# Attention in a decoder layer: the weighing of V in two halves, and scores moved ahead of the last third of a slot's transpositions

## The chip, the cores and the metric

The kernel runs on one core of a Trainium2 chip. The metric is device time in microseconds; lower is better. A core has five engines: TensorE (PE; its weight loads are PEld), VectorE (DVE), ScalarE (ACT), GpSimd (POOL) and SyncE (SP), which starts the DMAs.

## The reference

One decoder layer on x of 16 x 224 x 512: a Mamba block, cross-attention to a context of 750 keys, and a feed-forward net with binarised weights. The change is in the attention:

```python
qh = _split_heads(q @ Wq + bq)          # q: layer norm of x, 16 heads of depth 32
kh = _split_heads(k @ Wk + bk)
vh = _split_heads(v @ Wv + bv)
logits = jnp.einsum('bhqd,bhkd->bhqk', qh, kh) / jnp.sqrt(jnp.asarray(DEPTH, dtype=jnp.float32))
logits = logits + mask * NEG_INF_SCALE
attn = jax.nn.softmax(logits, axis=-1)
out = jnp.einsum('bhqk,bhkd->bhqd', attn, vh)
out = out.transpose(0, 2, 1, 3).reshape(B, Sq, D_MODEL)
return out @ Wo + bo
```

## The kernel before

Three phases follow each other: `mamba_phase` (which also makes keys and values and keeps them in DRAM), `attention_phase` and `ffn_phase`. In the attention phase everything is cut into slots, 16 to a batch of 224 queries, 256 in all. Each engine has a program of its own, written as a loop over the slots (L1222 for PE, L1325 for ACT, L1488 for DVE, L1559 for POOL, L1617 for SP), and semaphores tie them together. The order on an engine is the order in that loop; an instruction that waits holds up all behind it.

A slot n is one half (375) of the keys for a block of four heads and 112 queries, so two slots make a block and four slots a group of four heads with all 224 queries. In it:

- PE makes the scores (`scores`, L1136), four matmuls into the PSUM tile `sps`, once the masks of the slot before have read that tile.
- DVE adds the mask, negates, and keeps the minimum (`negate_and_mask`, L1394), four instructions from `sps` into `sc`, one of two buffers that blocks take in turn. Before it writes a block's first half, it waits until PE has transposed all of the block two before (L1401). After the odd slot it makes `nmax`, the maximum over both halves.
- ACT makes the exponentials in place, two a slot (`exponential`, L1282), one for each head of a block. The first of a block needs `nmax`, so it can only start in the odd slot after its masks.
- PE transposes two heads' probabilities two slots later in three parts of four transpositions (`transpose_p(m, pair)`, L1150; here a part is called a third). Two PSUM buffers `tps` take the thirds in turn, so each third waits for the copy of the one before last. ACT copies the first and the last third to `pT`, DVE the middle one (`keep_pT`, L1293 and L1412). The first third needs one of the two heads' exponentials, the others both.

Beside these stand units that share two more PSUM banks `ups` in turn: `project_q` (L1126, one for each group, copied by ACT in `keep_q`), `weigh_v` (L1175, 24 matmuls over all keys of a group; it waits until ACT and DVE have copied all the group's thirds), `spread_sums` (L1167, the reciprocal sums, copied by ACT in `keep_sums`), `out_proj` (L1189, two a batch, added to x by DVE) and `transpose_h` (L1108, the normalised x of the next batch). The layer norm of the next batch runs over four engines: statistics on DVE (`stats_of_x1`), a logarithm and an exponential on ACT (`guess_rsqrt`, L1268), four small instructions on POOL (`rsqrt_of_rows`), and the scaling on DVE (`normalise`, L1375), ahead of which DVE waits.

By slot of a batch, r0 to r15, PE had: Q in r1, r5, r9, r13; a weighing with its sums in r2, r6, r10, r14; an output projection in r4 and r7 (of the batch before); the transpositions of h in r12; nothing beside the scores and the thirds in r0, r3, r8, r11, r15. The order in a slot was scores, first third, Q or weighing, middle third, h, sums or output projection, last third.

## Time and profile before

| | us |
|---|---|
| median of 3 runs | 3591.51 (3588.01 to 3595.86) |
| profiled execution | 3588.75 |
| its span | 3587.4 |
| PE busy in the span | 3224.2 (90%) |
| DVE busy | 2655.8 (74%) |
| ACT busy | 2388.7 (67%) |
| POOL busy | 1806.3 (50%) |

The mean granted clock of TensorE is 0.963 of full speed. In a timeline each line is one instruction, or several alike in a row (x8), with its start and length; the bracket at the end says how long the engine stood still before it and what released it. A matmul in float32 shows as two instructions. The lengths of matmuls overlap, so the price of a unit is read from its start to the start of the next one.

### The profile page before, as it was taken

The numbers are of one execution on the slowest core, as the hardware profiler recorded it, in microseconds if no ns is written. First come the engines' busy times: TensorE is split into PE (matmuls) and PEld (weight loads), VectorE is DVE, ScalarE is ACT, GpSimd is POOL, SyncE is SP. The second block draws the span as 40 slices with busy tenths as digits, with TensorE's granted clock in tenths as the row PEclk, the third lists the DMA queues.
The fourth block names the chain that finished last, engine by engine and source line by source line (L and its number), as shares of the span: only waits on it lengthen the run. The fifth ranks groups of instructions, "written<-read, shape, count | busy, mean of one in ns | idle before, by whom it ended". The sixth has DMA issues, their size and how long they took to land. (4 is left out here: it accounts for less than half of the span.)

```text
span 3587.4 us, 59841 instructions
## 1 busy us (share of the span) xinstructions
PE 3224.2 (90%) x20864; PEld 2259.3 (63%) x20864; DVE 2655.8 (74%) x4671; ACT 2388.7 (67%) x5339; POOL 1806.3 (50%) x1213
## 2 busy tenths in 40 slices
PE   5798989898898988988997998999999999999998
PEld 4566655665566655666554666666666666678787
DVE  2899999999999999999984776767766677622221
ACT  5777788777877788777863667666666667522221
POOL 2778887888878888888873000000000000055554
PEclk8899999999999999999998999999999999999999
DMA  5667666666666666676564041111211121020110
GB/s 166 162 175 196 188 167 157 184 175 188 168 161 182 190 171 160 175 196 180 159 166 155 6 124 59 46 46 65 71 46 46 51 78 66 18 76 24 36 35 24
DMA packets 286234, 425.03 MB, mean 118 GB/s; under 512 B 28689, under 2 KB 226065, under 8 KB 281330
## 3 DMA queue, kind: packets, MB, share of 16 engines
q1 hardware_dynamic: 278573, 411.44, 41.1%
q10 hardware_dynamic: 7365, 9.77, 0.9%
q8 instruction: 170, 2.79, 0.3%
q14 instruction: 126, 1.03, 0.1%
HBM read 320.12 MB, written 101.02 MB: 117 GB/s over the span
## 5 line engine op out<-in xcount | busy, mean ns | idle before, releaser
L810 POOL TENSOR_TENSOR a_hs<-a_rep,a_bmat 128x896 f32<-128x896 f32 x512 | 1061.0, 2094 | 291.0 <-PE a_yps L322 290.7
L442 ACT ACTIVATE a_states<-a_rep,a_a_neg 128x224 f32<-128x224 f32 x2048 | 793.5, 437 | 103.0 <-DVE a_hs L706 101.5
L699 DVE TENSOR_TENSOR_SCAN a_states<-a_states,a_hs 128x900 f32<-128x900 f32 x384 | 779.6, 2030 | 72.7 <-ACT a_states L442 57.9
L1403 DVE CUSTOM_DVE_ANT_0 b_sc<-sps,early_mask 112x375 f32<-112x375 f32 x1024 | 500.0, 545 | 154.1 <-PE sps L1146 153.9
L1162 PEld LDWEIGHTS b_tps<-ident,b_sc 112*125 112x125 f32 x3072 | 402.0, 191 | 286.4 <-issue 168.7
L1162 PE MATMUL b_tps<-ident,b_sc 112*125 112x112 f32 x3072 | 491.4, 289 | 77.3 <-DVE b_pT L1417 36.2
L1289 ACT ACTIVATE b_sc<-b_sc,b_nmax 112x750 f32<-112x750 f32 x512 | 467.4, 914 | 62.5 <-DVE b_nmax L1409 62.3
L1545 POOL TENSOR_SCALAR b_x_var<-mv 112x2 f32<-112x2 f32 x16 | 3.4, 213 | 889.2 <-DVE mv L1454 889.2
L344 PE MATMUL a_work<-early_scan_hT,w_in 128*128 128x224 f32 x2048 | 424.3, 363 | 8.9 <-issue 6.3
L706 DVE TENSOR_TENSOR a_hs<-a_states,a_cmat 128x896 f32<-128x896 f32 x384 | 419.2, 1092 | 13.2
L344 PEld LDWEIGHTS a_work<-early_scan_hT,w_in 128*128 128x128 f32 x2048 | 395.5, 196 | 49.1 <-issue 42.2
L1298 ACT ACTIVATE b_pT<-b_tps 125x448 f32<-125x448 f32 x512 | 272.5, 535 | 135.9 <-PE b_tps L1162 134.7
L399 PE MATMUL a_work<-ctx,a_wk 128*128 128x250 f32 x1536 | 347.8, 379 | 14.3 <-ACT kv_out L489 14.3
L403 PE MATMUL a_work<-wv,ctx 128*125 128x512 f32 x768 | 349.6, 598 | 9.6 <-ACT kv_out L486 8.9
L322 PE MATMUL a_yps<-a_hs,a_fold 128*32 128x224 f32 x4096 | 236.4, 373 | 115.2 <-POOL a_hs L817 46.1
L399 PEld LDWEIGHTS a_work<-ctx,a_wk 128*128 128x128 f32 x1536 | 288.8, 191 | 64.8 <-issue 16.7
L374 PE MATMUL a_work<-a_w_out,a_yT 128*112 128x512 f32 x512 | 255.5, 657 | 33.5 <-DVE early_du L689 33.5
L1779 ACT ACTIVATE c_g<-sps,early_b,early_alpha 128x512 f32<-128x512 f32 x112 | 87.1, 778 | 287.7 <-PE sps L1719 282.5
L699 DVE TENSOR_TENSOR_SCAN a_hs<-a_states,a_hs 128x900 f32<-128x900 f32 x128 | 258.9, 2023 | 24.1 <-ACT a_states L442 24.1
L322 PEld LDWEIGHTS a_yps<-a_hs,a_fold 128*32 128x32 f32 x4096 | 129.9, 113 | 223.9 <-DVE a_hs L706 101.7
L1815 DVE CAST c_gT_hi<-c_g 128x512 fp32r<-128x512 f32 x112 | 61.8, 552 | 278.3 <-ACT c_g L1779 278.3
L1849 POOL TENSOR_TENSOR c_gT_lo<-c_g,c_gT_hi 128x512 fp32r<-128x512 f32 x112 | 146.4, 1309 | 212.9 <-DVE c_gT_hi L1815 212.9
(194 smaller groups left out, 5011.4 us busy)
## 6 DMA issues: line engine op xcount, KB each, us to landing
a_rep<-du_scratch SPq DMA_DIRECT2D x512, 224.0 KB, 5.7
w_in<-W_in_dram SPq DMA_DIRECT2D x128, 512.0 KB, 4.4
du_scratch<-early_du SPq DMA_DIRECT2D x16, 1792.0 KB, 11.5
ctx<-ctxT_dram SPq DMA_DIRECT2D x48, 500.0 KB, 6.0
v_scratch<-kv_out SPq DMA_DIRECT2D x96, 250.0 KB
k_scratch<-kv_out SPq DMA_DIRECT2D x96, 250.0 KB, 4.5
b_keys<-k_scratch SPq DMA_DIRECT2D x8, 1500.0 KB, 8.6
b_v<-v_scratch SPq DMA_DIRECT2D x8, 1500.0 KB
```

The costliest lines, as they stand in the source:

```text
L322: mm = pe.matmul(yps[j * DG:(j + 1) * DG, tile % 2 * L:(tile % 2 + 1) * L], fold[:], hs[(G4 * tile + j) % RING][:, q, 1:ROW], start=(q == ...
L344: mm = pe.matmul(work[:, bank, j * L:(j + 1) * L], w_in[unit % WINS][:, k, j * P:(j + 1) * P], hT[:, k, :], start=(k == 0), stop=(k == KD ...
L399: mm = pe.matmul(work[:, bank, j * WIDE:(j + 1) * WIDE], wk[:, k, (2 * half + j) * P:(2 * half + j + 1) * P], keys[:, k, :], start=(k == 0 ...
L403: mm = pe.matmul(work[0:KC, bank, :], keys[:, k, half * KC:(half + 1) * KC], wv[:, k, :], start=(k == 0), stop=(k == KD - 1))
L442: e = act.activation(rows(states[:, g % DA, :])[:, q, 1:ROW], rep[tile % REPS][:, j, 0, :], ACT.Exp, scale=a_neg[:, g % SLOTS, q:q + 1])
L699: dve.tensor_tensor_scan(state if g % G4 else whole, state, whole, 0.0, ALU.mult, ALU.add).then_inc(S["scan"], 1)
L706: dve.tensor_tensor(hh[:, :, 1:ROW], rows(states[:, g % DA, :])[:, :, 1:ROW], cmat[b % 2][:], ALU.mult).then_inc(S["hc"], 1)
L810: pool.tensor_tensor(hs[g % RING][:, :, 1:ROW], rep[tile % REPS][:, j, 1, :].unsqueeze(1).broadcast_to([P, Q, L]), bmat[b % 2][:], ALU.mul ...
L1162: mm = pe.transpose(tps[0:KC, tile % 2, c * TT:(c + 1) * TT], sc[m // 2 % 2][:, 2 * (m % 2) + head, chunk * KC:(chunk + 1) * KC], ident[0: ...
L1289: act.activation(sc[block % 2][:, j, :], sc[block % 2][:, j, :], ACT.Exp, scale=-1.0, bias=nmax[:, block % 2, j:j + 1], accum_out=esum[:, ...
L1298: act.activation(place(m, pair), transposed(tile), ACT.Copy).then_inc(S["pt_act"], 1)
L1403: dve.tensor_tensor_reduce(out=sc[block % 2][:, j, cols], in0=sps[0:TT, j, 0:HALF], in1=mask[:, block % 2, cols], scale=-1.0, scalar=3.0e3 ...
```

## The change

On PE a slot's order becomes: scores, last third of the slot before (`transpose_p(slot - 3, 2)`), first third, Q, half a weighing, middle third, h, sums or output projection. `weigh_v` is cut in two halves of three key chunks each: the first in r2, r6, r10, r14 takes the bank and makes the waits, the second follows one slot later and signals. With it `spread_sums`, `keep_sums` and `scale_o` move by one slot. The second output projection moves from r7 to r8, the projection of Q of the next batch's first group from r13 to r14, the transpositions of h from r12 to r13, and the statistics, layer norm, stores and loads that go with them by one slot each.

On ACT the last third's copy moves into the next slot, ahead of the first third's copy. In even slots one exponential now comes ahead of both. `guess_rsqrt(b)` moves from r11, where it stood ahead of both exponentials, to r12, where it stands behind both. No instruction is added or removed. The core of the diff:

```diff
@@ -1056,7 +1058,8 @@
         FT = F // P
         T = 4 * P
         LAST = (B - 1) * SLOTS
-        ROWS_AT = (LAST + 13, LAST + 15, LAST + 16, LAST + 17)
+        ROWS_AT = (LAST + 12, LAST + 13, LAST + 16, LAST + 17)
+        Q_AT = (-2, 1, 5, 9)
         tps = mem.psum("tps", [P, 2, BANK])
         ups = mem.psum("ups", [P, 2, BANK])
 
@@ -1069,7 +1072,7 @@
             "x2_var", "x2_log", "x2_guess", "x2_rstd", "biases", "const", "alpha2", "alpha2_row", "s1", "mv_in0", "mv_in1",
             "rows_in", "w2_in", "w2", "rows", "rows_hi", "rows_lo", "f_ps")
 
-        slots = range(-6, B * SLOTS + SLOTS // 2 + 4)
+        slots = range(-6, B * SLOTS + SLOTS // 2 + 5)
         unit_of, bank_of = {}, {}
 
         def loads(b):
@@ -1172,19 +1175,22 @@
                                    ident[0:TT, 0:TT], start=True, stop=True)
                 signal(("r", G, 0), mm)
 
-            def weigh_v(b, g):
+            def weigh_v(b, g, part):
                 G = b * GROUPS + g
-                bank = take_bank(("pv", G, 0), "oT", G + 1)
-                pe.wait_ge(S["pt_act"], 2 * GROUP * (G + 1))
-                pe.wait_ge(S["pt_dve"], GROUP * (G + 1))
-                if b:
-                    pe.wait_ge(S[f"v{b % 2}"], 16 * loads(b))
-                for c in range(CHUNKS):
+                if part == 0:
+                    take_bank(("pv", G, 0), "oT", G + 1)
+                    pe.wait_ge(S["pt_act"], 2 * GROUP * (G + 1))
+                    pe.wait_ge(S["pt_dve"], GROUP * (G + 1))
+                    if b:
+                        pe.wait_ge(S[f"v{b % 2}"], 16 * loads(b))
+                bank = bank_of["pv", G, 0]
+                for c in range(part * CHUNKS // 2, (part + 1) * CHUNKS // 2):
                     for j in range(GROUP):
                         mm = pe.matmul(ups[j * DH:(j + 1) * DH, bank, 0:L],
                                        v[b % 2][:, c, (g * GROUP + j) * DH:(g * GROUP + j + 1) * DH],
                                        pT[G % 2][:, :, j * CHUNKS + c, :], start=(c == 0), stop=(c == CHUNKS - 1))
-                mm.then_inc(S["pv"], 1)
+                if part:
+                    mm.then_inc(S["pv"], 1)
 
             def out_proj(b, i):
                 bank = take_bank(("o", b, i), "x2", 2 * b + i + 1)
@@ -1227,29 +1233,34 @@
                     spread_alpha()
                 if 0 <= slot < N_ALL:
                     scores(slot)
+                if 3 <= slot <= N_ALL + 1:
+                    transpose_p(slot - 3, 2)
                 if before:
                     transpose_p(slot - 2, 0)
                 for b in range(B):
                     at = slot - b * SLOTS
-                    if -3 <= at < -3 + SLOTS and (at + 3) % 4 == 0:
-                        project_q(b, (at + 3) // 4)
-                    if 6 <= at < 6 + SLOTS and (at - 6) % 4 == 0:
-                        weigh_v(b, (at - 6) // 4)
+                    if at in Q_AT:
+                        project_q(b, Q_AT.index(at))
+                for b in range(B):
+                    at = slot - b * SLOTS
+                    for part in range(2):
+                        if 6 <= at - part < 6 + SLOTS and (at - part - 6) % 4 == 0:
+                            weigh_v(b, (at - part - 6) // 4, part)
                 if before:
                     transpose_p(slot - 2, 1)
+                if slot == N_ALL + 1:
+                    transpose_p(slot - 2, 2)
                 for b in range(B):
                     at = slot - b * SLOTS
-                    if at == -4 and b:
+                    if at == -3 and b:
                         transpose_h(b, 0)
                         transpose_h(b, 1)
-                    if 6 <= at < 6 + SLOTS and (at - 6) % 4 == 0:
-                        spread_sums(b * GROUPS + (at - 6) // 4)
+                    if 7 <= at < 7 + SLOTS and (at - 7) % 4 == 0:
+                        spread_sums(b * GROUPS + (at - 7) // 4)
                     if at == SLOTS + 4:
                         out_proj(b, 0)
-                    if at == SLOTS + 7:
+                    if at == SLOTS + 8:
                         out_proj(b, 1)
-                if before:
-                    transpose_p(slot - 2, 2)
                 if slot in ROWS_AT:
                     transpose_rows(ROWS_AT.index(slot))
             for f in range(3):
@@ -1329,31 +1340,33 @@
                 if slot - LAST - 10 in range(4):
                     sign_w2(slot - LAST - 10)
                 ready = 1 <= slot <= N_ALL
+                if ready and slot % 2 == 0:
+                    exponential(2 * slot - 2)
+                if 3 <= slot <= N_ALL + 1:
+                    keep_pT(slot - 3, 2)
                 if before:
                     keep_pT(slot - 2, 0)
-                if ready and slot % 2 == 0:
-                    exponential(2 * slot - 2)
                 for b in range(B):
                     at = slot - b * SLOTS
-                    if -3 <= at < -3 + SLOTS and (at + 3) % 4 == 0:
-                        keep_q(b * GROUPS + (at + 3) // 4)
+                    if at in Q_AT:
+                        keep_q(b * GROUPS + Q_AT.index(at))
+                if ready:
+                    exponential(2 * slot - 1 - slot % 2)
                 for b in range(B):
                     at = slot - b * SLOTS
-                    if at == -5 and b:
+                    if at == -4 and b:
                         guess_rsqrt(b)
-                    if at == -4 and b:
+                    if at == -3 and b:
                         keep_hT(b, 0)
                         keep_hT(b, 1)
-                    if 6 <= at < 6 + SLOTS and (at - 6) % 4 == 0:
-                        keep_sums(b * GROUPS + (at - 6) // 4)
-                    if at == SLOTS + 9:
+                    if 7 <= at < 7 + SLOTS and (at - 7) % 4 == 0:
+                        keep_sums(b * GROUPS + (at - 7) // 4)
+                    if at == SLOTS + 10:
                         guess_rsqrt_x2(b)
-                if ready:
-                    exponential(2 * slot - 1 - slot % 2)
-                if before:
-                    keep_pT(slot - 2, 2)
                 if ready and slot % 2:
                     exponential(2 * slot - 1)
+                if slot == N_ALL + 1:
+                    keep_pT(slot - 2, 2)
                 if slot in ROWS_AT:
                     keep_rows(ROWS_AT.index(slot))
             act.preload_act_table_set("gelu_and_others")
@@ -1497,19 +1510,19 @@
                     fold_bv()
                 for b in range(B):
                     at = slot - b * SLOTS
-                    if 7 <= at < 7 + SLOTS and (at - 7) % 4 == 0:
-                        scale_o(b, (at - 7) // 4)
+                    if 8 <= at < 8 + SLOTS and (at - 8) % 4 == 0:
+                        scale_o(b, (at - 8) // 4)
                 if 0 <= slot < N_ALL:
                     negate_and_mask(slot)
                 for b in range(B):
                     at = slot - b * SLOTS
-                    if at == -6 and b:
+                    if at == -5 and b:
                         stats_of_x1(b)
-                    if at == -5 and b:
+                    if at == -4 and b:
                         normalise(b)
                     if 6 <= at < 6 + SLOTS and (at - 6) % 4 == 0:
                         invert_sums(b, (at - 6) // 4)
-                    if at == SLOTS + 8:
+                    if at == SLOTS + 9:
                         row_stats(b)
                 if before:
                     keep_pT(slot - 2)
@@ -1517,9 +1530,9 @@
                     at = slot - b * SLOTS
                     if at == SLOTS + 4:
                         add_residual(b, 0)
-                    if at == SLOTS + 7:
+                    if at == SLOTS + 8:
                         add_residual(b, 1)
-                if slot == LAST + 11:
+                if slot == LAST + 10:
                     normalise_rows()
                 if slot in ROWS_AT:
                     split_rows(ROWS_AT.index(slot))
@@ -1559,11 +1572,11 @@
             for slot in slots:
                 for b in range(B):
                     at = slot - b * SLOTS
-                    if at == -6 and b:
+                    if at == -5 and b:
                         rsqrt_of_rows(b)
-                    if at == -6:
+                    if at == -5:
                         add_bo(b)
-                    if at == SLOTS + 8:
+                    if at == SLOTS + 9:
                         rsqrt_of_x2(b)
 
         def sync_program():
@@ -1622,19 +1635,19 @@
                 if slot == LAST + 4:
                     load_rows()
                     load_w2()
-                if slot == LAST + 12:
+                if slot == LAST + 13:
                     load_mv(4, ready, "mv_in1")
                 for b in range(B):
                     at = slot - b * SLOTS
                     if at == -6 and b:
                         load_k(b)
-                    if at == -8 and b:
+                    if at == -7 and b:
                         load_x1(b)
                     if at == -4 and b:
                         load_v(b)
-                    if at == SLOTS + 8:
+                    if at == SLOTS + 9:
                         store_x2(b)
-                    if at == SLOTS + 11:
+                    if at == SLOTS + 12:
                         store_stats(b)
             sp.wait_ge(S["mv_in1"], 16)
             sp.wait_ge(S["stats_out"], 16 * B)
```

## Rows read from the trace of the kernel before

**Rows 1.** Busy time by engine in the attention stage; then PE's granted clock, DMA share, GB/s.
```profile
1954.90:3137.10 1182.20, 1090.19 (x9369) 747.69 (x9369) 812.02 (x2887) 794.02 (x1766) 69.95 (x182) 0.97 0.18 58
```

**Rows 2.** Timeline, slots r3 and r4: start us, length us, engine, line, operation, [idle before].
```profile
2405.76 0.90 PE L1146 MATMUL sps<-early_keys,b_q 32*112 32x375 f32 x8
...
2406.59 2.07 PE L1162 MATMUL b_tps<-ident,b_sc 112*125 112x112 f32 x12
2406.73 0.55 DVE L1403 CUSTOM_DVE_ANT_0 b_sc<-sps,early_mask 112x375 f32<-112x375 f32 x1 [0.46 <-PE sps L1146]
...
2407.32 0.54 ACT L1298 ACTIVATE b_pT<-b_tps 125x448 f32<-125x448 f32 x1 [0.20 <-PE b_tps L1162]
...
2407.98 0.51 PEld L1162 LDWEIGHTS b_tps<-ident,b_sc 112*125 112x125 f32 x4 [0.23 <-issue]
...
2408.84 0.90 PE L1146 MATMUL sps<-early_keys,b_q 32*112 32x375 f32 x8 [0.17 <-DVE b_half_min L1403]
2408.92 0.92 ACT L1289 ACTIVATE b_sc<-b_sc,b_nmax 112x750 f32<-112x750 f32 x1 [1.06 <-DVE b_nmax L1409]
...
2409.84 0.52 ACT L1298 ACTIVATE b_pT<-b_tps 125x448 f32<-125x448 f32 x1
...
2409.99 0.69 PE L1162 MATMUL b_tps<-ident,b_sc 112*125 112x112 f32 x4 [0.25 <-ACT b_sc L1289]
2410.26 0.91 ACT L1289 ACTIVATE b_sc<-b_sc,b_nmax 112x750 f32<-112x750 f32 x1
...
2411.32 0.69 PE L1162 MATMUL b_tps<-ident,b_sc 112*125 112x112 f32 x4 [0.64 <-ACT b_sc L1289]
...
2411.84 3.60 PE L1193 MATMUL b_ups<-early_wo,b_oT 128*112 128x512 f32 x8
```

**Rows 3.** Timeline of slots r5 and r6: projection of Q, weighing, sums.
```profile
2415.80 0.90 PE L1146 MATMUL sps<-early_keys,b_q 32*112 32x375 f32 x8
...
2417.15 1.69 PE L1132 MATMUL b_ups<-early_hT,early_wq 128*128 128x224 f32 x8
...
2418.68 1.02 PE L1162 MATMUL b_tps<-ident,b_sc 112*125 112x112 f32 x8
...
2418.88 0.45 ACT L1279 ACTIVATE b_q<-b_ups,early_bq 128x224 f32<-128x224 f32 x1 [0.99 <-PE b_ups L1132]
...
2420.47 0.69 PE L1162 MATMUL b_tps<-ident,b_sc 112*125 112x112 f32 x4
...
2421.08 2.48 PE L1184 MATMUL b_ups<-b_pT,early_v 125*32 125x224 f32 x48
...
2424.02 0.61 PE L1171 MATMUL b_ups<-ident,b_rwide 112*128 112x112 f32 x4
...
2424.66 0.36 ACT L1304 ACTIVATE b_rb<-b_ups 128x224 f32<-128x224 f32 x1 [1.77 <-PE b_ups L1171]
```

**Rows 4.** Timeline of r9 and of r11 to r12, behind DVE's other work.
```profile
2436.01 0.66 PE L1162 MATMUL b_tps<-ident,b_sc 112*125 112x112 f32 x4 [1.09 <-DVE b_pT L1417]
...
2446.49 0.20 ACT L1270 ACTIVATE early_guess<-early_var_eps 112x2 f32<-112x2 f32 x1
...
2449.03 0.62 DVE L1417 COPY b_pT<-b_tps 125x448 f32<-125x448 f32 x1
...
2449.80 1.10 PE L1162 MATMUL b_tps<-ident,b_sc 112*125 112x112 f32 x8 [1.21 <-DVE b_pT L1417]
```

**Rows 5.** PE's timeline: scores of r0 twice, r2 twice; a window's busy times and clock.
```profile
2027.51 0.90 PE L1146 MATMUL sps<-b_keys,b_q 32*112 32x375 f32 x8 [0.17 <-DVE b_half_min L1403]
...
2400.41 0.90 PE L1146 MATMUL sps<-early_keys,b_q 32*112 32x375 f32 x8
...
2471.72 0.90 PE L1146 MATMUL sps<-b_keys,b_q 32*112 32x375 f32 x8
...
2973.28 0.90 PE L1146 MATMUL sps<-early_keys,b_q 32*112 32x375 f32 x8 [0.17 <-DVE b_half_min L1403]
...
2549.00:2561.00 12.00, 10.86 (x53) 5.87 (x49) 5.94 (x20) 6.43 (x15) 0.00 (x0) 0.86 0.00 0
```

## The prediction

> **What bounds the kernel now.** I read the granted clock and the busy shares by stage first, then the timeline of all engines over one batch of the attention stage, then PE's waits in it. The change touches only that stage, which runs from 1954.9 to 3137.1 us of the trace [rows 1]. There PE is busy 1090 of 1182 us, DVE 812 and ACT 794: PE carries the stage, and what can be won or lost is the time in which it stands still. One batch is 16 slots. Undisturbed it takes 71.31 us from one slot's scores to the same slot's of the next batch (2400.41 to 2471.72) [rows 5]. I number a batch's slots r0 to r15; even slots hold the first half of a block's keys, odd ones the second.
>
> Two loops pace a slot. The first is scores, masks, scores: 3.08 us from 2405.76 to 2408.84 [rows 2]. Of it 0.97 lies between the scores' start and the first mask, and 2.11 between that and the next scores. The second starts only in an odd slot, because the block's maximum is complete only then: the first exponential starts 2.19 us after that slot's first mask (2406.73 to 2408.92), so 3.15 to 3.16 us after its scores. The even slot that follows transposes what these exponentials made, and PE waits 0.25 and 0.64 us for them [rows 2]. PE's other larger waits are for DVE's copy of the middle third: 1.09 us in r9 behind the row statistics and 1.21 in r12 behind the layer norm of the next batch [rows 4].
>
> **Prices.** On PE [rows 2, 3]: scores 0.83, a third of the transpositions 0.52 (2411.32 to 2411.84; 0.61 ahead of a weighing, 2420.47 to 2421.08), projection of Q 1.53 (2417.15 to 2418.68), weighing 2.42 (2421.08 to 2424.02, less one third), sums 0.44 (the 0.61 of the row less 0.17, by which a third's 0.69 overlaps what follows it), output projection 3.44 (2411.84 to 2415.80, less one third). The transpositions of h, twice the instructions of the sums, I put at 0.8. Between engines: a third's start to its copy on ACT 0.73 (2406.59 to 2407.32), copy's start to the buffer's reuse 0.66 (2407.32 to 2407.98); exponential's start to the transposition that needs it 1.07; projection of Q to its copy 1.73, that copy to the next instruction 0.35 (its 0.45 less the 0.10 by which copies overlap), the sums' copy likewise 0.26; sums to their copy 0.64. On ACT one exponential takes 0.92 and one copy 0.42 (2408.92, 2409.84, 2410.26).
>
> **The change, part by part.** No instruction is added or taken away, and apart from 0.09 us for each restart of a weighing the work on PE stays: 16 x (0.83 + 3 x 0.52) + 4 x (1.53 + 2.42 + 0.44) + 2 x 3.44 + 0.8 = 63.5 us a batch. What changes is the order.
>
> *Halves.* A weighing of 2.42 becomes 1.2 + 1.2 in an even and the following odd slot, and the sums move with the second. An odd slot so filled costs 0.83 + 0.52 + 0.61 + 1.2 + 0.52 + 0.44 = 4.12. Before, r3, r11 and r15 held 2.39 of work in 3.08 us, and so did r8, which now takes the second output projection. That frees 4 x 0.69 = 2.8 us a batch, and is the gain of the change together with the 1.09 of r9.
>
> *Scores ahead of the last third.* Here stand two new waits. First, the masks of an even slot write into the buffer of two blocks before, and wait until PE has transposed it, up to the slot three back. Its last third now comes after the scores. It starts at 0.83, the masks at 0.83 + 0.73 = 1.56 instead of 0.97, and the next scores at 3.67 instead of 3.08 at the earliest. Second, and larger: ACT's program in an even slot now has an exponential ahead of the last third's copy. Behind that exponential are queued this copy, the copy of the first third and the last exponential. The first half of the weighing waits for that very copy; in a slot without weighing the middle third waits for it too, since it needs the buffer. So in every even slot PE cannot go on before 3 x 0.92 + 0.66 = 3.42 us after the odd slot's first exponential.
>
> Replay of one batch by the prices, each slot's time from its own scores:
> - r1, Q: 0.83 + 0.52 + 0.52 + 1.53 + 0.52 = 3.92. Q's copy is ahead of the exponential: 1.87 + 1.73 + 0.35 = 3.95.
> - r2, first half: weighing possible at 3.95 + 3.42 - 3.92 = 3.45, wanted at 1.96: stall 1.5. Length 3.45 + 1.2 + 0.52 = 5.17.
> - r3, second half and sums: 4.12. Sums are copied at 3.68 + 0.64 = 4.32 and the second exponential follows at 4.58.
> - r4, output projection: last third's copy done at 4.58 + 0.92 + 0.92 + 0.66 - 4.12 = 2.96, middle third wanted at 1.87: stall 1.1. Length 2.96 + 0.52 + 3.44 = 6.92. Together 20.13 for r1 to r4, and the same for r5 to r8.
> - r9, r10, r11 as r1 to r3: 13.21. The row statistics' wait of 1.09 is gone: they now run in r9, and its projection of Q hides them. If that cover fails it is back: 15 x 1.1 = 16 us.
> - r12, nothing beside: 3.67 by the masks. The layer norm's logarithm and exponential now stand behind ACT's last exponential, at 2.30 + 0.42 + 0.42 + 0.92 = 4.06. Rows 4 have 2.54 from this to DVE's copy of the middle third, so 6.60, which is 2.93 into r13.
> - r13, transposition of h: first third at 2.93 + 0.77 = 3.70 instead of 1.35 (stall 2.35); masks at 2.93 + 0.54 = 3.47, next scores at 5.58.
> - r14, Q and first half: r13's first exponential starts at 3.47 + 2.19 = 5.66, then come two copies of h and two exponentials, so the weighing is possible at 5.66 + 0.84 + 3.42 - 5.58 = 4.34; length 6.06.
> - r15 4.12, r0 3.67. Together 19.43 for r13 to r0.
>
> The batch comes to 20.13 + 20.13 + 13.21 + 3.67 + 19.43 = 76.57 against 71.31: 5.26 us more, with 13 us of standing still instead of 8. Fifteen such periods make 79 us. The first slots and the tail hold the same work in the same order of dependence; I take them at nothing, bounded by one period's 5.3 on either side. The DMAs moved by a slot each stay ahead of their readers, for they are moved with them: the load of x1 is one slot later, as is its first reader.
>
> **The clock.** In the thirteen periods from 2027.51 to 2973.28 a batch takes 72.75 on average [rows 5], 18.7 us above 13 x 71.31. In this time the granted clock falls ten times from 2.4 to 1.2 GHz for some microseconds, each time after PE's waits in r4, r9, r12 or r0 (one stands in rows 5, a mean of 0.86 over 12 us). That is 1.87 us for each. The new order has eight waits of 1.1 us and more a batch where there were two, so I take one more fall a batch, 15 x 1.87 = 28 us; the bounds are none and four.
>
> Sum: 3588.75 (profiled execution, span 3587.4) + 79 + 28 = 3695.8; the median of the runs is 2.8 us above that execution, so **3698**.
>
> **Rivals.**
> *A, the forecast:* ACT's queue sets the even slots; 3640 to 3740.
> *B, the clock falls in half of the new waits:* four falls a batch instead of 0.75, 3.25 x 1.87 x 15 = 91, so 3588.75 + 79 + 91 + 2.8 = 3762. For it speaks that r12 and r13 put 1.1 and 2.35 of idle close together. Against it: with three or four such places a batch in thirteen periods, only ten brought a fall. The Trainium skill (TensorE: Matmul & The Clock Gate, "A second HAM failure mode: psum-queue depth-cycling") tells of a kernel whose short idles between matmul groups made the clock swing between its levels. By that rule the time is this rival's 3762; the trace agrees so far that each fall follows a wait.
> *C, faster:* the last third's copy does not stand in the way. If ACT reached it before PE wants the weighing, the slots would be 3.92, 3.68, 4.12, 5.83 twice, then 3.92, 3.68, 4.12, 3.67 and 3.2, 5.2, 4.12, 3.67: 66.7 a batch, 4.6 less, 15 x 4.6 = 70 and 3521. It would need that copy 1.2 us earlier in the even slots on average; at 0.7 us earlier it breaks even. For it speaks that ACT is busy only 67% of the stage; against it that its time is idle while it waits for the maximum and full right after. The Trainium skill (Perfetto Trace Analysis, "Optimization Strategy") holds that interleaving stretches with different limits may help. By that rule the time is this rival's 3521, and the idle 0.17 and 0.89 of the slots without weighing agree.
> *D, half of it:* the stalls come but are shorter, as ACT catches up in slots with an output projection; 3585 to 3640.
>
> **How the numbers follow.** A 0.64, B 0.12, C 0.11, D 0.13, of which 0.05 within 0.2% and 0.08 slower. Two tenths of a per cent, 7 us, is about what a measurement of this kernel can tell from no change. So faster 0.11, same 0.05, slower 0.84. The range takes all of A, most of B and the upper half of D: 3605 to 3790.
>
> **What would show it.** Right: periods of about 76.6 us where the clock is full; PE waits at the weighing's line for ACT's copy, some 1.5 us in r2, r6 and r10; about 1.1 at the middle third in r4 and r8; 2.3 for DVE in r13; the even slots' masks 1.56 after their scores. Wrong: if ACT's copy of the last third starts less than 1.8 us into even slots, or PE comes to the weighing later than this copy is done, the time lies near C. If r13 is under 4 us long, the layer norm's chain was mis-sized, worth 15 x 1.7 = 26 us.

## The result, and the profile after

The changed kernel takes 3688.45 us (median of 4 runs, 3684.07 to 3690.01) against 3593.2 for the kernel before (4 runs): a ratio of 1.0266, 95% interval 1.0252 to 1.028. The forecast was 3698 in a range of 3605 to 3790, slower with a chance of 0.84. The profiled execution took 3686.97 us, 98.2 more than that of before.

The head of the page after, with the busy shares and the clock over the 40 slices:

```profile
span 3685.6 us, 59841 instructions
...
PE 3245.3 (88%) x20864; PEld 2266.3 (61%) x20864; DVE 2656.5 (72%) x4671; ACT 2391.1 (65%) x5339; POOL 1806.7 (49%) x1213
...
PEclk8899999999999999999998989999999999999999
```

DVE, ACT and POOL are busy as long as before, PE 21 us longer (3224.2 to 3245.3); the rest of the 98 us is PE standing still. Busy time by window: one period of 16 slots (of the eighth batch), 12 us of r13 and r14 of the seventh, and the attention stage (columns as in rows 1):

```profile
2511.70:2590.24 78.54, 68.37 (x586) 46.42 (x585) 50.63 (x181) 49.10 (x110) 4.50 (x12) 0.96 0.16 52
...
2494.00:2506.00 12.00, 9.78 (x64) 7.24 (x65) 6.57 (x25) 7.11 (x17) 3.28 (x6) 0.72 0.27 103
...
1951.00:3235.00 1284.00, 1110.11 (x9365) 752.21 (x9365) 812.96 (x2887) 795.34 (x1766) 69.83 (x182) 0.95 0.16 53
```

The stage is about 100 us longer than in [rows 1]: from the first scores of the first batch to those of the last it is 1186.07 us against 1085.82. A usual period is now 78.51 us, against 71.32 (the most frequent one, without a fall of the clock). PE's waits in the period of the first window:

```profile
PE b_ups L1189 <- issue: 4.1, 3, 1.4
PE b_tps L1165 <- ACT b_pT L1309: 3.5, 4, 0.9
PE b_tps L1165 <- DVE b_pT L1430: 1.6, 1, 1.6
PE sps L1149 <- DVE b_half_min L1416: 1.0, 2, 0.7
```

L1189 is the weighing, L1165 a third, L1149 the scores; the numbers are us in all, times, longest. This window is of the one batch whose wait for DVE in r13 is 1.6; in the others it is 1.92, and r13's scores wait 0.35 less. The waits of [rows 2] for exponentials are gone from this list, and so is the 1.09 of r9 in [rows 4]; the wait behind the layer norm, 1.21 in r12 before, stands in r13 and is longer. The others are new. "Issue" at the weighing means that the profile names no releaser; the weighing's own waits, and the timeline, point at ACT's copy of the last third. The timeline shows where they lie; slot r2 (scores at 2440.78) and slot r4 (2450.26):

```profile
2440.78 0.90 PE L1149 MATMUL sps<-early_keys,b_q 32*112 32x375 f32 x8
2440.81 0.91 ACT L1300 ACTIVATE b_sc<-b_sc,b_nmax 112x750 f32<-112x750 f32 x1
...
2441.61 1.13 PE L1165 MATMUL b_tps<-ident,b_sc 112*125 112x112 f32 x8
...
2441.72 0.91 ACT L1300 ACTIVATE b_sc<-b_sc,b_nmax 112x750 f32<-112x750 f32 x1
...
2442.62 0.91 ACT L1300 ACTIVATE b_sc<-b_sc,b_nmax 112x750 f32<-112x750 f32 x1
...
2443.52 0.95 ACT L1309 ACTIVATE b_pT<-b_tps 125x448 f32<-125x448 f32 x2
...
2444.14 1.34 PE L1189 MATMUL b_ups<-b_pT,b_v 125*32 125x224 f32 x24 [1.41 <-issue]
...
2450.26 0.90 PE L1149 MATMUL sps<-early_keys,b_q 32*112 32x375 f32 x8
...
2451.09 1.12 PE L1165 MATMUL b_tps<-ident,b_sc 112*125 112x112 f32 x8
...
2451.95 0.55 DVE L1416 CUSTOM_DVE_ANT_0 b_sc<-sps,early_mask 112x375 f32<-112x375 f32 x1 [0.75 <-PE b_tps L1165]
...
2453.10 0.66 PE L1165 MATMUL b_tps<-ident,b_sc 112*125 112x112 f32 x4 [0.89 <-ACT b_pT L1309]
```

In r2 the last third is transposed at 2441.61, but ACT runs three exponentials one after the other and copies that third only at 2443.52; the weighing starts 0.62 after the copy does. In r4 the same copy holds up the middle third. The masks of r4 start 1.69 us after its scores, 0.86 after the last third's start.

Then r13 and the start of r14, behind the layer norm:

```profile
2494.43 0.90 PE L1149 MATMUL sps<-early_keys,b_q 32*112 32x375 f32 x8 [0.30 <-DVE b_half_min L1416]
...
2494.55 0.20 ACT L1281 ACTIVATE early_guess<-early_var_eps 112x2 f32<-112x2 f32 x1
...
2495.89 0.19 POOL L127 TENSOR_TENSOR early_rstd<-early_tmp,early_guess 112x2 f32<-112x2 f32 x1
...
2496.18 1.00 DVE L1394 TENSOR_SCALAR early_ln<-b_xt,early_mv,early_rstd 112x512 f32<-112x512 f32 x2 [1.90 <-issue]
...
2497.10 0.62 DVE L1430 COPY b_pT<-b_tps 125x448 f32<-125x448 f32 x1
...
2497.86 1.99 PE L1165 MATMUL b_tps<-ident,b_sc 112*125 112x112 f32 x8 [1.92 <-DVE b_pT L1430]
...
2501.28 1.61 PE L1149 MATMUL sps<-early_keys,b_q 32*112 32x375 f32 x8
```

The logarithm and exponential stand behind ACT's last exponential, POOL and DVE follow, and PE waits 1.92 us. Eight matmuls then take 1.99 us instead of 1.10 [rows 4] and the scores 1.61 instead of 0.90: TensorE is at 1.2 GHz, and the granted clock is 0.72 over the 12 us from 2494.00. From the second batch to the fifteenth all but the fourth have the same 0.96 over the period, with this one fall; the fourth is taken up below. The kernel before had ten falls in thirteen periods, but shorter ones: the one in [rows 5] takes 0.14 off the clock of 12 us, this one 0.28, so half clock lasts twice as long.

### The profile page after: what moved, and what is told of

Same layout as the page of the kernel before. It is cut to its first block and busy times, and to the rows that moved or that the text cites. A ratio compares the mean times of both kernels' runs of the same rounds, so it can differ in the third digit from the quotient of the medians.

```text
span 3685.6 us, 59841 instructions
## 1 busy us (share of the span) xinstructions
PE 3245.3 (88%) x20864; PEld 2266.3 (61%) x20864; DVE 2656.5 (72%) x4671; ACT 2391.1 (65%) x5339; POOL 1806.7 (49%) x1213
## 5 line engine op out<-in xcount | busy, mean ns | idle before, releaser
L1165 PEld LDWEIGHTS b_tps<-ident,b_sc 112*125 112x125 f32 x3072 | 396.5, 196 | 298.0 <-issue 191.3
L1165 PE MATMUL b_tps<-ident,b_sc 112*125 112x112 f32 x3072 | 478.9, 294 | 90.8 <-ACT b_pT L1309 61.5
L1309 ACT ACTIVATE b_pT<-b_tps 125x448 f32<-125x448 f32 x512 | 250.7, 537 | 346.7 <-PE b_tps L1165 346.6
L1430 DVE COPY b_pT<-b_tps 125x448 f32<-125x448 f32 x256 | 158.4, 619 | 155.4 <-PE b_tps L1165 153.9
```

The costliest lines, as they stand in the source:

```text
L1165: mm = pe.transpose(tps[0:KC, tile % 2, c * TT:(c + 1) * TT], sc[m // 2 % 2][:, 2 * (m % 2) + head, chunk * KC:(chunk + 1) * KC], ident[0: ...
L1309: act.activation(place(m, pair), transposed(tile), ACT.Copy).then_inc(S["pt_act"], 1)
```

## The experiments

The table gives the time of a slot from its scores to the next, in us, as the median over twelve batches, and in the last rows the usual period, the mean of 14 periods and the granted clock of the whole program. Slots r5, r6 and r7 are as r1, r2 and r3 (but before: r7 5.95, r8 3.07; *ahead*: r5 3.84), r11 and r15 as r3 (but *best*: r11 4.41). The kernel before took 3579.4 us (one run) on the chip of *first*, *norm*, *halves* and *ahead*, 3593.75 on that of *first + norm*, *even*, *halves + norm* and *whole*, and 3591.79 on that of *best* and the last two kernels. Where no range is given, the kernel ran once. The names: *first* = ACT copies the last third first, *norm* = `guess_rsqrt` early, *halves* = halved weighing with the last third back at the slot's end, *ahead* = last third moved, weighing whole, *whole* = neither, norm early, *even* = first and norm, and the last third ahead of the scores in even slots, *best* = halves, norm and `row_stats` behind the copy.

| slot | before | after | first | norm | first + norm | even | halves | ahead | halves + norm | whole | best |
|---|---|---|---|---|---|---|---|---|---|---|---|
| r1 | 3.84 | 3.84 | 3.84 | 3.84 | 3.84 | 4.28 | 3.84 | 6.69 | 3.84 | 3.84 | 3.84 |
| r2 | 5.36 | 5.26 | 4.35 | 5.25 | 4.35 | 3.92 | 3.78 | 6.83 | 3.78 | 5.36 | 3.77 |
| r3 | 3.08 | 4.22 | 4.23 | 4.22 | 4.23 | 4.66 | 4.22 | 3.08 | 4.22 | 3.07 | 4.22 |
| r4 | 6.96 | 6.86 | 6.27 | 6.87 | 6.27 | 5.53 | 6.08 | 7.50 | 6.08 | 6.96 | 6.08 |
| r8 | 3.07 | 6.87 | 6.27 | 6.86 | 6.27 | 5.53 | 6.08 | 7.50 | 6.08 | 6.97 | 6.08 |
| r9 | 4.97 | 3.84 | 3.84 | 3.84 | 3.84 | 4.28 | 3.84 | 3.84 | 3.84 | 3.84 | 3.84 |
| r10 | 5.50 | 5.25 | 4.35 | 5.25 | 4.35 | 3.91 | 4.34 | 6.84 | 4.34 | 5.92 | 3.78 |
| r12 | 4.46 | 3.80 | 3.80 | 3.80 | 3.80 | 3.07 | 3.20 | 4.07 | 3.20 | 4.65 | 3.08 |
| r13 | 3.84 | 6.85 | 7.16 | 3.60 | 3.60 | 4.04 | 8.34 | 7.21 | 3.79 | 4.73 | 3.91 |
| r14 | 5.36 | 6.17 | 6.33 | 5.91 | 5.41 | 4.98 | 8.00 | 7.34 | 5.77 | 7.14 | 5.77 |
| r0 | 3.59 | 3.80 | 3.80 | 3.80 | 3.80 | 3.08 | 3.08 | 4.36 | 3.07 | 3.59 | 3.08 |
| period | 71.32 | 78.51 | 75.09 | 75.01 | 70.60 | 69.43 | 71.97, later 75.09 | 83.2 to 89.3 | 68.30 | 74.9 to 75.3 | 67.92 |
| mean | 72.65 | 79.23 | 75.59 | 75.93 | 71.12 | 69.96 | 74.19 | 86.75 | 68.63 | 75.75 | 68.32 |
| clock | 0.963 | 0.954 | 0.955 | 0.966 | 0.967 | 0.970 | 0.955 | 0.936 | 0.968 | 0.955 | 0.970 |

**First: is it ACT's order in even slots?** The changed kernel, with the last third's copy ahead of the exponential (in the diffs, "..." stands for lines left out):

```diff
+                if 3 <= slot <= N_ALL + 1:
+                    keep_pT(slot - 3, 2)
                 if ready and slot % 2 == 0:
                     exponential(2 * slot - 2)
-                if 3 <= slot <= N_ALL + 1:
-                    keep_pT(slot - 3, 2)
```

> The changed kernel with one swap on ScalarE: in even slots the copy of the last third comes ahead of the exponential. Queue theory (PE's waits in even slots are for this copy behind three exponentials): the copy comes one exponential, 0.92 us, sooner, so r2, r6, r10 go from 5.26 to 4.34 us, r4 and r8 from 6.86 to 5.94, r14 loses 0.7, r0 and r12 stay at 3.80 by the masks; a batch goes from 78.51 to 73.2 us and the time to about 3609. Rival, masks and exponentials limit the even slots by themselves: nothing moves, 3688.

Measured: 3633.7 us (before on the same chip 3579.4), period 75.09, where 73.2 was expected. Slots r2, r6 and r10, with a first half, went from 5.25 to 4.35, as expected. The rest of the miss is in three places: r14 did not lose 0.7 but grew by 0.16, r13 grew by 0.31, and slots r4 and r8 fell to 6.27 and stayed 0.3 over what was expected. The timeline of r4 shows a wait that the replay had not seen:

```profile
2508.13 1.12 PE L1165 MATMUL b_tps<-ident,b_sc 112*125 112x112 f32 x8
...
2508.86 0.54 ACT L1309 ACTIVATE b_pT<-b_tps 125x448 f32<-125x448 f32 x1 [0.19 <-PE b_tps L1165]
...
2509.55 0.66 PE L1165 MATMUL b_tps<-ident,b_sc 112*125 112x112 f32 x4 [0.29 <-ACT b_pT L1309]
```

A third's way to its copy and back takes 0.73 + 0.69 us, while PE's two thirds take 1.13: with nothing between first and middle third, 0.29 is lost even if ACT is free. ACT's order carries 3.4 us of the 7.2 a period. The fall of the clock in r13 remains.

**Norm: is it the layer norm's place?** `guess_rsqrt` comes first on ACT in r12 instead of behind both exponentials:

```diff
+                for b in range(1, B):
+                    if slot - b * SLOTS == -4:
+                        guess_rsqrt(b)
                 if ready and slot % 2 == 0:
                     exponential(2 * slot - 2)
...
-                    if at == -4 and b:
-                        guess_rsqrt(b)
```

> The changed kernel with the layer norm's logarithm and exponential ahead of all else on ScalarE in r12, not behind both exponentials. Chain theory: r13 falls from 6.85 to about 3.3 us and r12 grows by 0.1. If the clock's fall in each batch comes from the waits in r12 and r13 together, it goes as well: a batch 74.9 us and about 3634. If it comes from the new waits in general, it stays somewhere in the batch: 76.8 us and about 3662. Rival, the chain was not what DVE waited for: 78.5 and 3688.

Measured: 3640.52 us, period 75.01, almost to the tenth. PE in r13, and the busy times and clock of a period:

```profile
2852.22 0.90 PE L1149 MATMUL sps<-b_keys,b_q 32*112 32x375 f32 x8
2853.04 2.07 PE L1165 MATMUL b_tps<-ident,b_sc 112*125 112x112 f32 x12
2854.95 0.93 PE L1116 MATMUL b_ups<-ident,early_ln 112*128 112x112 f32 x8
2855.81 0.90 PE L1149 MATMUL sps<-b_keys,b_q 32*112 32x375 f32 x8
```
```profile
2790.94:2865.94 75.00, 66.17 (x585) 44.85 (x584) 50.46 (x181) 48.79 (x110) 4.50 (x12) 1.00 0.16 55
```

No wait in r13, and the clock is full, though PE still waits 4.5 us in four places at the weighing (1.4 the longest) and 3.9 in four at a third behind ACT's copy (1.2 the longest). Eleven of the fifteen periods are like this one. Falls are left in the first and the fourth batch, and one short one each in the sixth, in r13 (period 75.66), and in the seventh (76.64). So the fall that came in every batch hung on the wait in r13 and not on the new waits at large, though these bring one now and then.

**First + norm.** Both edits.

> The changed kernel with both repairs: copy of the last third ahead of the exponential, and the layer norm's functions first in r12. Queue theory, the two add: 75.1 - 3.6 - 0.4 = 71.1 us a batch, about level with the kernel before (ratio near 1.00). Rival, they overlap: the chain of r12 and r13 returns by another way and a batch stays above 73.

Measured: 3555.5 us, period 70.60. Together they take away 7.9 us a period, more than 3.4 and 3.5, since r14 gains as well (6.17 to 5.41), which it had not done in *first*, where the clock fell ahead of it. In this form the change is below the kernel before by 0.7 a period.

**Halves: one part alone.** On PE and ACT the last third goes back to the end of its slot (ACT again has the first third's copy ahead of the even slot's exponential); halves and shifted units stay.

```diff
-                if 3 <= slot <= N_ALL + 1:
-                    transpose_p(slot - 3, 2)
                 if before:
                     transpose_p(slot - 2, 0)
...
                         out_proj(b, 1)
+                if before:
+                    transpose_p(slot - 2, 2)
```

> The changed kernel with the last third back at the end of its own slot on PE and ScalarE (scores not ahead), halves and shifted units kept. Queue theory: r1 to r4 become 3.84, 3.68, 4.15, 6.2 us; r13 keeps its wait for the layer norm, 5.9 us; a batch 70.0 us, with a fall of the clock 71.9, and a time near the kernel before, 3560 to 3590. Rival, the halves cost (shift of the sums and units): a batch stays above 76 us and the time above 3650.

Measured: 3603.01 us, over the 3560 to 3590 expected. The period is 71.97 from the second batch to the seventh but for the fourth, as expected with a fall of the clock, then 75.09. The reason is again the layer norm, worse than in the change itself: PE waits 3.19 us, and half clock follows. The wait is the same in every batch; what differs is how long half clock lasts, three times as long in the thirteenth batch as in the second (a clock of 0.63 and of 0.88 over 14 us). The longer stretch costs 3.1 us a period. Why it lasts longer in the later batches stays open.

```profile
2083.31 1.32 PE L1165 MATMUL b_tps<-ident,b_sc 112*125 112x112 f32 x8 [3.19 <-DVE b_pT L1426]
...
2896.64 1.99 PE L1165 MATMUL b_tps<-ident,b_sc 112*125 112x112 f32 x8 [3.19 <-DVE b_pT L1426]
...
2900.89 1.61 PE L1149 MATMUL sps<-early_keys,b_q 32*112 32x375 f32 x8
```
```profile
2082.00:2096.00 14.00, 12.69 (x115) 9.68 (x116) 9.03 (x35) 8.03 (x17) 2.51 (x2) 0.88 1.03 234
2895.00:2909.00 14.00, 12.36 (x76) 9.63 (x77) 7.02 (x25) 6.76 (x14) 2.50 (x2) 0.63 0.18 69
```

**Ahead: the other part alone.** The weighing is whole again, in the even slot, with its sums; the last third stays behind the scores.

```diff
-                        if 6 <= at - part < 6 + SLOTS and (at - part - 6) % 4 == 0:
+                        if 6 <= at < 6 + SLOTS and (at - 6) % 4 == 0:
...
-                    if 7 <= at < 7 + SLOTS and (at - 7) % 4 == 0:
-                        spread_sums(b * GROUPS + (at - 7) // 4)
+                    if 6 <= at < 6 + SLOTS and (at - 6) % 4 == 0:
+                        spread_sums(b * GROUPS + (at - 6) // 4)
```

> The changed kernel with the weighing whole again in the even slot, its sums and scaling back with it; scores stay ahead of the last third. Queue theory: the weighing waits as long as before for the copy and nothing fills the odd slots: r2 6.9, r3 3.08, r4 7.5 us, a batch about 82.7 us, 3750. Rival, the halves are what costs: a batch near 72 us and 3590.

Measured: 3799.97 us, mean period 86.75, slower than expected (82.7). The slots r2, r3 and r4 came out as expected (6.83, 3.08, 7.50); the excess is where the clock falls. The granted clock over the 86.75 us from 2400.00 is 0.86, with three falls in it, in r4, r12 and the next r0. They take 0.14 off, where the one fall of the changed kernel takes 0.04 off a period. This is near what rival B had foreseen for the change itself.

**Halves + norm.** The two edits that had helped, without the moved third.

> Halves without scores ahead, and the layer norm's logarithm and exponential ahead of the rest in r12 (both single edits together). By the slots measured: r1 to r4 17.9 us, r5 to r8 17.9, r9 to r12 15.6, r13 3.3, r14 5.3, r15 4.2, r0 3.1: a batch 67.3 us against 71.3 of the kernel before, and hardly a fall of the clock, so 60 to 80 us under the kernel before, a ratio of 0.978 to 0.984. Rival: the scores-ahead order carries part of the gain and without it a batch stays above 70: ratio 0.99 or more.

Measured: 3522.48 us (3515.72 to 3524.03) against 3593.75, ratio 0.9804, interval 0.9781 to 0.9826. The period is 68.30 and the clock over one is 1.00.

**Even: last third ahead of the scores in even slots.** First + norm, and in even slots only PE again transposes the last third first, so that the masks need not wait.

```diff
+                if 3 <= slot <= N_ALL + 1 and slot % 2 == 0:
+                    transpose_p(slot - 3, 2)
                 if 0 <= slot < N_ALL:
                     scores(slot)
-                if 3 <= slot <= N_ALL + 1:
+                if 3 <= slot <= N_ALL + 1 and slot % 2:
                     transpose_p(slot - 3, 2)
```

> As the kernel with both repairs, and in even slots the last third stands ahead of the scores again, so that the masks need not wait for it; in odd slots it stays behind the scores. Theory that the masks' wait is real and worth 0.7 us where nothing else fills the slot: r0 and r12 fall from 3.80 to about 3.1, a batch to about 69.7. Rival, the masks' wait is hidden in all slots: r0 and r12 stay at 3.8.

Measured: 3539.78 us, period 69.43. Slots r0 and r12 drop from 3.80 to 3.08: the masks' new wait for the last third was worth 0.72 in each. The odd slots give part of it back (r1 and r9 4.28 instead of 3.84, r3 4.66 instead of 4.23), and 1.2 a period is left.

**Whole: neither part.** Weighing whole and last third at the slot's end, with only the shifts of the other units and the early norm.

> Neither halves nor scores ahead, only the shifted units and the layer norm's functions first in r12. It isolates what the halves are worth. Theory: halves fill the odd slots, so without them r3, r7, r11 and r15 are 3.08 and r2, r6, r10 and r14 2.42 to 1.2 longer: a batch about 71.5 us, level with the kernel before. Rival, the shift of the units alone brings the gain: a batch near 67.5.

Measured: 3630.51 us, period 74.9 to 75.3, where 71.5 was expected. Against halves + norm r2, r6 and r10 are 1.58 longer each, but r3, r7, r11 and r15 1.15 shorter, so a weighing's two slots gain only about 0.4 by halving. Slots r4 and r8 gain 0.88 each, because behind a filled odd slot PE no longer waits for exponentials. The surprise is in r12 to r14, with 16.5 us against 12.8. A look at PE in the batch with r12 at 4.16 and one with r12 at 4.65:

```profile
2467.08 1.10 PE L1165 MATMUL b_tps<-ident,b_sc 112*125 112x112 f32 x8 [1.28 <-DVE b_pT L1427]
...
2540.26 1.10 PE L1165 MATMUL b_tps<-ident,b_sc 112*125 112x112 f32 x8 [1.28 <-DVE b_pT L1427]
...
2542.73 1.61 PE L1149 MATMUL sps<-b_keys,b_q 32*112 32x375 f32 x8
```

PE waits 1.28 us in r12 for DVE, which makes the statistics of the layer norm ahead of its copy; with halves r11 is 1.15 longer and hides part of them. Half clock follows in the second of the two batches and not in the first, which had its fall in r8, 20 us earlier. And r14 carries a projection of Q and a whole weighing. The output projection in r8 instead of r7 costs 1.0 (r7 and r8 together 10.04 instead of 9.02), since in r8 PE waits for exponentials ahead of it. So the shifts lose 4 us a period, and halving returns 7, some of both through the clock: a usual period of *whole* has one fall, one of halves + norm none. The "shifts" here take in one more difference in ACT's order that all these kernels share and none tests alone: an exponential ahead of the copies of the sums and of h, where the kernel before had it behind them.

**Best: row statistics behind the copy.** In halves + norm PE's two largest waits were for DVE, 0.66 in r13 and 0.52 in r10. DVE's `row_stats(b)` goes behind its copy of the middle third in r9:

```diff
-                    if at == SLOTS + 9:
-                        row_stats(b)
                 if before:
                     keep_pT(slot - 2)
                 for b in range(B):
                     at = slot - b * SLOTS
+                    if at == SLOTS + 9:
+                        row_stats(b)
```

> Halves without scores ahead and the layer norm's functions first in r12, and besides VectorE's row statistics in r9 behind its copy of the middle third. Theory: r10 of that kernel, 4.34 us against 3.78 of r2 and r6, waits for this copy and falls to 3.9 at most; a batch goes from 68.30 to 67.9 and the time down by 6 us, ratio to the kernel before about 0.979. Rival, the statistics then delay the masks of r10 by as much: a batch stays at 68.3.

Measured: 3514.81 us (3512.49 to 3515.53), ratio 0.9785, interval 0.9771 to 0.98. Slot r10 lost 0.56 and r11 gained 0.19. By its period this is the best of all, though its interval overlaps that of halves + norm; it is 2.2% below the kernel before and 4.7% below the change. A period of it and PE's waits in it:

```profile
2496.66:2564.58 67.92, 66.04 (x585) 44.58 (x584) 50.44 (x180) 49.16 (x111) 4.50 (x12) 1.00 0.18 60
```
```profile
PE b_tps L1165 <- DVE b_pT L1427: 0.6, 1, 0.6
PE b_tps L1165 <- ACT b_pT L1307: 0.4, 1, 0.4
PE b_ups L1135 <- ACT early_hT L1273: 0.2, 1, 0.2
PE sps L1149 <- DVE b_half_min L1413: 0.2, 1, 0.2
```

These waits come to 1.4 us in 68, where those of the changed kernel were 10.2.

**The fourth batch: signs of the weights on ACT.** Its period is 88.36 in the changed kernel, 9.85 over the usual one, and 75.06 in the kernel before, 3.74 over. `sign_w1` runs first on ACT in its r0 to r3. Its instruction and what PE does behind the first two:

```profile
2188.77 1.90 ACT L1319 ACTIVATE s<-raw_w 128x2048 fp32r<-128x2048 f32 x1
...
2192.14 0.70 PE L1165 MATMUL b_tps<-ident,b_sc 112*125 112x112 f32 x4 [2.68 <-ACT b_pT L1309]
2192.78 1.61 PE L1149 MATMUL sps<-b_keys,b_q 32*112 32x375 f32 x8
```

1.90 us is added ahead of a copy that was late already, and the clock falls. Two kernels spread the four signs over r3, r7, r11 and r15, behind ACT's first copy, in the best kernel and in the changed one:

```diff
-                if slot - 3 * SLOTS in range(KD):
-                    sign_w1(slot - 3 * SLOTS)
...
+                if slot - 3 * SLOTS in (3, 7, 11, 15):
+                    sign_w1((slot - 3 * SLOTS) // 4)
```

> As the kernel with the row statistics behind the copy, and the four signs on w1 in slots 51, 55, 59 and 63. Theory as for the changed kernel: the fourth batch, 72.9 us so far, comes to within 2 us of the others; 3 us less in all. Rival: it stays at 72.9.

> The changed kernel with the four sign instructions on w1 (ScalarE, 1.9 us each, in slots 48 to 51, the fourth batch) moved to slots 51, 55, 59 and 63, where ScalarE waits for the maximum. The fourth batch takes 88.4 us in the changed kernel against 78.5 in the others, and 75.1 against 71.3 in the kernel before. Theory: with ScalarE's queue on the path each sign lengthens its slot; spread into idle time the batch falls below 82. Rival, the fourth batch is long for another reason, such as the load of w1: it stays at 88.

Measured: 3518.05 us in the best kernel (3509.69 to 3524.56; ratio 0.9788, interval 0.9769 to 0.9807), no difference from 3514.81, and 3689.37 in the changed one, none from 3686.97. The fourth batch takes 74.0 where it was 72.39, and 82.32 where it was 88.36, but there the two behind it then take 82.71 and 80.44, and the three add up to 245.5, as before (245.6). Both expectations failed. That the signs bring the loss stands on the timeline, and their own delay did shrink: in the changed kernel r0 to r3 were 9.5 us over their usual length in all, and with the signs spread r4, r12 and the next r0 are 0.8, 0.4 and 0.4 over. What took its place are falls of the clock where a usual batch has none: in r8 (2.5 us over) and in r1 of the two batches behind (1.6 us each), the last of them behind waits of 0.89 and 0.30 us that stand in every batch. Why they come there stays open.

## Why the prediction was right, step by step

The experiments add up to a chain of single steps, in us a period: before 71.32; units shifted, norm early 75.2; halves 68.3; last third behind the scores 75.0; norm behind ACT's last exponential 78.5.

- **ACT's order in even slots.** Right in mechanism and nearly in size. The stalls of 1.5 in r2, r6 and r10 are 1.41, those of 1.1 in r4 and r8 0.89. Moving one copy ahead of one exponential gave back 3.4 us.
- **The masks' wait.** Right in kind, sized 0.13 too small. The masks start 1.69 to 1.70 after the scores instead of 1.56. I had taken ACT's 0.73 from a third's start to its copy; for DVE's masks it is 0.87. Slots r0 and r12 are 3.80 instead of 3.67.
- **Halved weighing.** Right in sign. Odd slots are 4.22 instead of 4.12: restarts and ends of units cost a little more than I took. r9's 1.09 is gone, as said.
- **The shifted units.** Beside the norm I gave them no price of their own. With a whole weighing they lose about 4 us a period (1.0 of it by the output projection in r8, most of the rest in r12 to r14 with the clock), and the halves are what hides them.
- **Layer norm in r12 and r13.** Right in mechanism: the wait is 1.92 us where I had 2.35, and it was worth 3.5 us a period with its fall. But r13 is 6.85 long and not 5.58, because the clock fell there every time.
- **The clock.** I took one more fall a batch at 1.87 us, 28 in all. Both factors were too large. A usual batch has one fall, always in r13, where the kernel before had 0.77 on average; and one costs about 1.4 us, an estimate from the measured 13.02 us of r13 and r14 against the 11.64 of the replay (1.65 if the replay is given r13's masks where they were measured, 3.20 after the scores and not 3.47). My 1.87 came from an excess of 18.7 us over ten falls, and 3.74 of this was the signs' batch, which I had not set apart; without it 15.0 us in thirteen periods, 1.15 a period or 1.7 for each of the other nine falls, and a period with one fall shows 1.6 directly (lines below). The term measures 15 x (1.4 - 1.15) = 4 us, or 7 with 1.65, and then the order of the work 4 less. That a fall costs no more here, though half clock lasts twice as long, would fit that PE no longer waits in r14, where *norm* has 0.44 us; this is not shown. Rival B's rule, half clock after many of the short idles, came true in the kernel *ahead*, with three falls in the period looked at, and not in this one.
- **The first slots and the tail.** I took them at nothing beside a bound of 5.3. This missed the signs' batch, which lies in neither: 6.1 us more than before (9.85 against 3.74).

Two periods of the kernel before, with one fall and with none:

```profile
2320.06:2392.97 72.91, 67.62 (x584) 46.69 (x585) 50.57 (x182) 48.96 (x110) 4.49 (x12) 0.98 0.17 56
2400.41:2471.72 71.31, 66.13 (x585) 45.43 (x584) 50.56 (x181) 48.95 (x111) 4.49 (x12) 1.00 0.17 57
```

The sum in the two executions: the order of the work, 78.51 less 1.4 for the clock less 71.32, is 5.8 a period, 87 us where I had 79; the clock 4 instead of 28; the signs 6 instead of nothing. That makes 97 of the measured 98.2, against my 107. That the total came so near is luck: one term too large by 24 covered two too small by 8 and 6. What the forecast had right shows in the usual period: 76.57 forecast at full clock, 77.1 measured with the 1.4 taken off (an estimate, as the 1.4 is).

Rival C is the instructive one. It put a period with the copy out of the way at 66.7. With the copy moved ahead and the norm early it was 70.60: the slots with a first half took 4.35 where C had 3.68, and r4 and r8 6.27 where it had 5.83, because the thirds' round trip through ACT holds PE up even then (0.29 in r4, 0.51 at the weighing of r2). No kernel with the moved third beat the same kernel without it (70.60 and 69.43 against 68.30). The rule cited there of the Trainium skill (Perfetto Trace Analysis, "Optimization Strategy"), that interleaving stretches with different limits may help, is borne out by the halved weighing alone (75.2 to 68.3 us a period).

## What to carry to other kernels

When work moves on the engine that sets the time, follow its small consumers too: here a 0.54 us copy queued behind an exponential, on an engine that is idle over a third of the time, cost 3.4 of the 7.2 us a period that the change lost. Test the parts of a compound change one by one: here, with the norm early, one part was worth 7 us a period and the other lost the same. A chain over several engines, such as a layer norm's, is worth a look in every queue it crosses: two 0.20 us instructions behind ACT's exponentials instead of ahead of them cost 3.5 us a period.

## What the runs showed of the hardware

The clock does not fall at each wait of a given length. With seven waits of about 0.9 to 1.4 us a period left in the kernel *norm* it stayed at 1.00 in eleven of fifteen periods, while the wait of 1.92 in r13 of the changed kernel (1.58 in one batch), with 0.30 and 0.88 shortly ahead of it, brought 1.2 GHz every time. In *whole* the same wait of 1.28 us in r12 was followed by half clock in one batch (the scores of 1.61 at 2542.73) and not in r12 of the batch before. Nor does half clock always last as long: behind the same wait of 3.19 us in *halves* the clock over 14 us was 0.88 in an early batch and 0.63 in a later one. The busy time of PE in a period shows the price directly: 66.2 us at full clock (the window of *norm*), 67.6 with one fall in the kernel before, 68.4 with one of twice the length in the changed kernel. What in the history ahead of a wait decides stays open.
